# Graph layers on one core: VectorE takes part of the next pair's columns later, the normalisation moves to the second tile, and two copies change places

## The chip, the cores and the metric

The kernel runs on one core of one Trainium2 chip, as one program. The metric is the time of that program on the device, in microseconds (us). The kernel before takes 2264.59 us (median of 3 runs, 2262.41 to 2264.99).

The core's engines are TensorE (PE in the profile, with PEld for its weight loads), VectorE (DVE), ScalarE (ACT), GpSimd (POOL) and SyncE (SP). Each runs its own instructions strictly in the written order and meets the others only at semaphores. SP and POOL also issue DMA transfers. What stands in front of an instruction on its own engine delays it as much as the semaphore that it waits for.

## The reference

Four graph layers follow each other over 10,000 nodes with 512 features and 2,500 edges, each with a residual and a layer norm. Their core is:

```
x = layernorm(x + GAT(x))        # two attention layers of width 1024, then "fc": h @ Wfc + bfc
x = layernorm(x + conv(x))       # relu(segment_sum((x @ W)[src] * edge_weight, dst))
x = layernorm(x + painn(x))      # messages on edges, softplus, two small products
x = layernorm(x + mlp(x))        # relu(concat(x[src], x[dst]) @ W.T + b), summed by src
```

The last three layers change only rows that an edge touches. All other rows of their output are layer norms of layer norms of the first layer's row.

## The kernel before

All nodes stand in 79 tiles of 128 rows, and two tiles make a pair (`m` in the code, one `s = m % 2` for its buffers). The second attention layer and the fc product with its norm are one long function, `node_layers`. The part that the change touches is the last third: a loop over 79 tiles `u`, which each of the five engines writes out for itself. In each tile PE makes the fc product in 8 slices `k` of three matmuls (lines 2653 to 2655, each operand split in a high and a low part, `x_hi` and `x_lo`). After each slice stands `beside(g)` with `g = 8u + k`: a table of positions, on each engine, at which the three edge layers are worked off beside the fc product. A conv step comes every 5 slices from tile 43 to tile 57, a painn step every 5 slices (in two parts, the second 3 slices later) from tile 58 to tile 74, and the mlp weights follow up to tile 78. The mlp layer itself runs after the loop.

What each engine does for the fc product and its norm:

- **Columns of the next pair.** From tile 40 on, the fc input of a pair comes ready for use from memory (`x_in`). ACT rounds a quarter of it to the high part (`round_columns`, line 2736, rows `g_x_hi<-g_x_in`) and DVE subtracts to get the low part (`split`, line 2930, rows `g_x_lo<-g_x_in`). Four such quarters `f` are made for pair m+1 while PE works at pair m. `fills(h)` puts all four in the first tile of pair m, at slices 0, 2, 4 and 6, on both engines. PE waits for all four low parts at the start of pair m+1, and SP loads new columns into the buffer when they are done.
- **Sum and statistics.** At the end of each tile DVE adds the residual rows (`add_rows`, line 3036, rows `fc_z`) and takes the statistics (3038). PE may start tile u+2 only after the addition of tile u. At the end of a pair DVE makes the variances (`spread`, 3046 to 3053).
- **Norm of the pair before.** In the first tile of pair m, ACT makes the reciprocal roots (`root`, lines 2797 and 2799) at slice 2, DVE the shifts (`results`, line 3060, and for pairs with edges also `y`, line 3070) at slice 2, and ACT the scaled rows at slice 7: two instructions of `normalize` (2808) for the 20 pairs with edges, or two of `finish_y` (2819) for the others.

A conv step (for edge tile n) on the engines: PE multiplies tile n (`product`, 1254 to 1256), turns n+1 and sums n+2. ACT at the same position rounds the turned sums of n+1 (`conv_t_hi`, 1284) and copies the sums of n+2 (1272, 1276). DVE adds tile n (`conv_z`, 1328), makes the low part of n+1 (`conv_t_lo`, 1349), and then statistics and variances of n (1332 to 1343). Three slices later ACT makes the root (1289, 1291), DVE the shift (`conv_shift`, 1355, 1356) and ACT three scaled rows (1301, 1302, 1304: `conv_x` twice and `conv_y`). PE's product of n+1 in the next step waits for `conv_t_lo` of n+1.

A painn step: in its first part PE makes features (1485, into the same PSUM tile as the sums, so only after ACT has copied these), ACT copies them (1552), DVE makes a mask (1628) and three message products (1640 to 1644) and, in every second step, `scalars` (1654) from the softplus. In its second part PE makes products and sums the edges (1496); ACT copies the hidden rows (1588), the turned rows (1544), in every second step the softplus (three instructions, 1596 to 1600), and then the edge sums (`copy_sums`, 1567, rows `painn_sums`).

Of the kernel before, what the change touches and what calls it, by code (L numbers as in the profile page):

```python
# [33 lines left out]
ET = -(-E // P)  # L34
# [11 lines left out]
S_X2DST, S_X2SRC, S_X3SRC, _, S_X3DST, S_OUT, S_EDGE = range(7)  # L46
# [1864 lines left out]
def node_layers(nc, sem, held, h1, al1, scan_row, row_d, row_s, map_d, map_s, slot_tab, b1, avec, h2, h2_cols, al2, bounce1, bounce2,  # L1911
# [67 lines left out]
    def takes_columns(m):  # L1979
        return m >= GM and rest(m)  # L1980
# [17 lines left out]
    def fills(h):  # L1998

        m = halves_of[h][0]  # L2000
        if m + 1 == MACROS:
# [2 lines left out]
        return [(k, f) for i, k, f in (((0, 2, 0), (0, 6, 1), (1, 2, 2), (1, 6, 3)) if slow else  # L2004
                                       ((0, 0, 0), (0, 2, 1), (0, 4, 2), (0, 6, 3))) if first_half[m] + i == h]

    def halves_done(m):
        return first_half[m + 1] if m + 1 < MACROS else HALVES

# [3 lines left out]
    with ExitStack() as ctx:  # L2013
# [241 lines left out]
        def with_x1(m):  # L2255
            return tiles(m)[0] < ENDS
# [10 lines left out]
        with nc.Block() as block:  # L2267
# [456 lines left out]
            def _(act):  # L2724
# [100 lines left out]
                def beside(g):  # L2825
# [23 lines left out]
                    if part == 1:  # L2849
                        if 0 <= n < ET:  # L2850
                            painn.copy_hidden(act, n)
                        if 0 <= n + 2 < ET:
                            painn.copy_xt(act, n + 2)
                        if 0 <= n < ET and n % 2 == 1:
                            painn.softplus(act, n // 2)
                        if 0 <= n + 1 < ET:
                            painn.copy_sums(act, n + 1)
                        if n % 2 == 0 and 0 <= n - 4 < ET:
                            painn.own(act, n - 4)
                            painn.own(act, n - 3)  # L2860
# [19 lines left out]
                for u in range(TILES):  # L2880
                    h = GH + u
                    m = halves_of[h][0]
                    if WFC < h <= WFC + KC:
                        round_fc(h - WFC - 1)
                    for k in range(KC):
                        for after_k, f in fills(h):
                            if after_k == k:
                                relu(m + 1, f)
                        if m > GM and h == first_half[m]:
                            if k == 2:  # L2890
                                root(m - 1)
                            if k == KC - 1 and with_x1(m - 1):
                                normalize(m - 1)
                            if k == KC - 1 and not with_x1(m - 1):
                                finish_y(m - 1)
                        beside(KC * u + k)
                root(MACROS - 1)
                for n in range(-1, ET):
# [13 lines left out]
            def _(dve):  # L2912
# [169 lines left out]
                def beside(g):  # L3082
# [21 lines left out]
                        conv.shifts(dve, n)  # L3104
                    n, part = painn_part(g)
                    if part == 0:
                        if n % 2 == 0 and 0 <= n - 2 < ET:
                            painn.scalars(dve, (n - 2) // 2)
                        if 0 <= n + 1 < ET:
                            if n == -1:  # L3110
                                dve.wait_ge(painn.w_scaled, 3)
                            painn.masks(dve, n + 1)
                            painn.messages(dve, n + 1)
                        if n % 2 == 0 and 0 <= n - 4 < ET:
                            painn.shifts(dve, (n - 4) // 2)
                            painn.far(dve, n - 4)
                            painn.far(dve, n - 3)
# [43 lines left out]
                for u in range(TILES):  # L3161
# [3 lines left out]
                        rest_fc(h - WFC - 1)  # L3165
                    for k in range(KC):
                        for after_k, f in fills(h):
                            if after_k == k:
                                split(m + 1, f)
                        if m > GM and h == first_half[m] and k == 2:  # L3170
                            results(m - 1)
                        beside(KC * u + k)
                    add_rows(h)
                    if h + 1 == halves_done(m):
                        spread(m)
# [103 lines left out]
```

How the kernel before makes its waits and increments, by code:

```python
            @block.sync  # L263
# [5 lines left out]
                def store(m, s):  # L269
                    for j in node_tiles(m):
                        sp.wait_ge(evac_done, 2 + 2 * m + j + 1)
                        sp.sem_inc(passed, 1)
                        sp.dma_start(h_out[bass.ds(m * G + j * P, P), :], h_sb[2 * s + j][:, :]).then_inc(h_stored[2 * s + j], 16)
                    n = len(node_tiles(m))
                    sp.wait_ge(al_done, 32 + 16 * m + 8 * n)
                    sp.sem_inc(passed, 1)
                    sp.dma_start(al_out[bass.ds(m * G, n * P), :].rearrange("(j p) k -> p j k", p=P),
                                 al_sb[s][:, 0:n, :]).then_inc(al_stored[s], 16)
# [1 line left out]
                def loop(start, stop):  # L280
                    with sp.Fori(start, stop) as i:
                        for s in range(2):
                            m = 2 * i + s
                            sp.wait_ge(lo_done, m + 1)
                            sp.sem_inc(passed, 1)
                            load(m + 2, s)
                            store(m, s)
# [7 lines left out]
                for k in range(2, KC):  # L296
                    sp.wait_ge(w_lo_done, 2 * (k - 1))
                    sp.dma_start(w_raw[:, k % 2, :], w[k * P:(k + 1) * P, :]).then_inc(w_in[k % 2], 16)
# [1 line left out]
                def load_w2(k):  # L301
                    if k >= 2:
                        sp.wait_ge(w2_lo_done, k - 1)
                    sp.dma_start(w_raw[:, k % 2, :], w2[k * P:(k + 1) * P, :]).then_inc(w2_in[k % 2], 16)
```

## Time and profile before

| | kernel before |
|---|---|
| time, median of 3 runs | 2264.59 us (2262.41 to 2264.99) |
| time of the profiled execution | 2264.73 us |
| span in the profile | 2263.0 us |
| PE busy | 2204.2 us, 97% |
| DVE busy | 1486.6 us, 66% |
| ACT busy | 1021.1 us, 45% |
| POOL busy | 943.2 us, 42% |
| PE's granted clock, mean | 0.99 |

The profile is one execution. Times in its views are counted from the start of the span. Matmuls are pipelined and their ends are modelled, so a row of 0.39 us on PE does not mean that the next matmul started that much later: the distance of the starts is what counts. "Idle before" in brackets is the time in which the engine had nothing to run before an instruction, with what ended it. The loop over the 79 tiles starts at 1475.1 us and its last tile ends near 2111.9 us; the conv steps lie between 1739 and 1911 us, the painn steps between 1922 and 2090 us.

### The profile page before, as it was taken

The page shows a single profiled execution, that of the slowest core. Times are in us where ns is not written, and L with a number is a line of the kernel's source. Part 1 is how long each engine was busy: PE and PEld are TensorE (multiplying, and loading weights), DVE is VectorE, ACT ScalarE, POOL GpSimd, SP SyncE. Part 2 cuts the span into 40 slices and gives each one's busy share as a digit, 9 for nine tenths or more (in the row PEclk, how much of TensorE's full clock was granted, in tenths as well). Part 3 has the DMA queues.
Part 4 walks back from the last instruction along what each step waited for, and adds up shares of the span by engine and source line. Part 5 has one row for each costly group of instructions (what it writes and reads, how often), then busy time and mean ns, then how long its engine had stood idle before and what let it go on. Part 6 is the DMA issues. An engine that isn't in the chain of part 4 may idle for free.

```text
span 2263.0 us, 36380 instructions
## 1 busy us (share of the span) xinstructions
PE 2204.2 (97%) x12269; PEld 1888.9 (83%) x12269; DVE 1486.6 (66%) x4615; ACT 1021.1 (45%) x2028; POOL 943.2 (42%) x931
## 2 busy tenths in 40 slices
PE   7999999979999999999999999999999999999997
PEld 6878888858899888888999999988888777888785
DVE  7777878754666856665335665277776766678675
ACT  4982113222366632222225665334344665666454
POOL 2018637645222234366542322023545553652542
PEclk9999999989999999999999999999999999999998
DMA  6343565443476757786225666356667776776542
GB/s 213 139 139 127 155 208 190 151 136 105 139 247 229 258 171 267 265 281 238 87 88 188 220 228 242 126 191 211 230 206 256 238 242 220 240 251 225 168 121 70
DMA packets 192495, 435.82 MB, mean 193 GB/s; under 512 B 45751, under 2 KB 74622, under 8 KB 191774
## 3 DMA queue, kind: packets, MB, share of 16 engines
q1 hardware_dynamic: 127034, 249.08, 31.8%
q0 software_dynamic: 65296, 184.67, 26.1%
q8 instruction: 89, 1.46, 0.3%
q14 instruction: 76, 0.62, 0.1%
HBM read 242.68 MB, written 190.96 MB: 192 GB/s over the span
## 4 chain that ended last, share of the span: by engine, by line
PE 70%; DVE 4%; ACT 2%; issue 2%; DMA 1%; POOL 0%; POOLq 0%; ACTq 0%; DVEq 0%; SPq 0%
PE g_h_ps L2611 7%; PE g_h_ps L2628 7%; PE g_h_ps L2613 7%; PE g_h_ps L2612 7%; PE g_h_ps L2629 6%; PE g_h_ps L2630 6%; PE g_h_ps L2653 5%; PE g_h_ps L2655 5%; PE g_h_ps L2654 5%; PE g_t_ps L80 4%; PE g_h_ps L1783 2%; PE g_h_ps L1785 2%; PE g_h_ps L1784 2%; PE g_sum_ps L1023 1%; PE g_sum_ps L1022 1%
## 5 line engine op out<-in xcount | busy, mean ns | idle before, releaser
L2750 ACT ACTIVATE g_act_t<-g_t_ps,g_b_col 128x256 f32<-128x256 f32 (+1 forms) x488 | 201.9, 466 | 395.0 <-PE g_t_ps L80 394.8
L2628 PE MATMUL g_h_ps<-g_x_hi,held_w_hi 128*128 128x256 f32 x1216 | 352.1, 290 | 0.0
L2629 PE MATMUL g_h_ps<-g_x_lo,held_w_hi 128*128 128x256 f32 x1216 | 343.9, 283 | 0.0
L2630 PE MATMUL g_h_ps<-g_x_hi,held_w_lo 128*128 128x256 f32 x1216 | 343.7, 283 | 0.0
L632 DVE CUSTOM_DVE_ANT_0 g_prod<-g_h_sb,g_a_rows 128x256 f32<-128x256 f32 x632 | 224.3, 420 | 84.7 <-ACT g_h_sb L513 75.6
L2653 PE MATMUL g_h_ps<-fc_w_hi,g_x_hi 128*128 128x512 f32 x632 | 268.4, 425 | 3.3 <-DVE fc_z L3036 2.5
L2611 PE MATMUL g_h_ps<-held_w_hi,g_x_hi 128*128 128x512 f32 x656 | 263.7, 402 | 0.0
L2612 PE MATMUL g_h_ps<-held_w_lo,g_x_hi 128*128 128x512 f32 x656 | 256.8, 391 | 0.0
L2613 PE MATMUL g_h_ps<-held_w_hi,g_x_lo 128*128 128x512 f32 x656 | 256.8, 391 | 0.0
L2655 PE MATMUL g_h_ps<-fc_w_hi,g_x_lo 128*128 128x512 f32 x632 | 247.3, 391 | 0.0
L441 PE MATMUL g_h_ps<-g_w_hi,g_x_hi 128*128 128x512 f32 x616 | 243.0, 395 | 3.9 <-DVE g_x_lo L618 2.0
L2654 PE MATMUL g_h_ps<-fc_w_lo,g_x_hi 128*128 128x512 f32 x632 | 246.7, 390 | 0.0
L442 PE MATMUL g_h_ps<-g_w_lo,g_x_hi 128*128 128x512 f32 x616 | 242.1, 393 | 0.0
L443 PE MATMUL g_h_ps<-g_w_hi,g_x_lo 128*128 128x512 f32 x616 | 241.9, 393 | 0.0
L2629 PEld LDWEIGHTS g_h_ps<-g_x_lo,held_w_hi 128*128 128x128 f32 x1216 | 232.7, 191 | 0.1
L2630 PEld LDWEIGHTS g_h_ps<-g_x_hi,held_w_lo 128*128 128x128 f32 x1216 | 232.7, 191 | 0.0
L2628 PEld LDWEIGHTS g_h_ps<-g_x_hi,held_w_hi 128*128 128x128 f32 x1216 | 232.4, 191 | 0.1
L2928 DVE CAST g_x_hi<-g_act_t 128x512 fp32r<-128x512 f32 (+1 forms) x244 | 104.4, 428 | 194.0 <-ACT g_act_t L2750 192.5
L513 ACT ACTIVATE g_h_sb<-g_h_ps 128x1024 f32<-128x1024 f32 x79 | 81.1, 1027 | 246.2 <-PE g_h_ps L443 231.4
L2946 DVE CUSTOM_DVE_ANT_0 g_prod<-g_h_sb,g_a_rows 128x256 f32<-128x256 f32 x320 | 116.7, 419 | 98.5 <-ACT g_h_sb L2770 98.4
L2930 DVE TENSOR_TENSOR g_x_lo<-g_act_t,g_x_hi 128x512 fp32r<-128x512 f32 (+1 forms) x244 | 168.3, 690 | 8.4
L2442 POOL DMA_INDIRECT g_x_in<-h,held_perm x99 | 100.5, 1016 | 173.5 <-PE g_t_ps L80 101.6
(401 smaller groups left out, 4839.4 us busy)
## 6 DMA issues: line engine op xcount, KB each, us to landing
h<-g_h_sb SPq DMA_DIRECT2D x120, 512.0 KB, 3.8
h<-g_rows_own SPq DMA_DIRECT2D x40, 512.0 KB, 4.8
g_x_in<-in_dram SPq DMA_DIRECT2D x39, 512.0 KB, 3.9
h_cols<-g_h_sb SPq DMA_DIRECT2D x38, 512.0 KB, 3.7
xb_rows<-in_dram SPq DMA_DIRECT2D x19, 1024.0 KB, 5.4
xb<-xb_rows SPq DMA_DIRECT2D x19, 1024.0 KB, 4.4
g_x_in<-h_cols SPq DMA_DIRECT2D x38, 512.0 KB, 6.9
g_x_in<-h SPq DMA_DIRECT2D x21, 512.0 KB, 5.5
```

Of the source, the lines that this page charges most:

```text
L441: pe.matmul(out, xh, wh, start=(k == 0), stop=False)
L442: pe.matmul(out, xh, wl, start=False, stop=False)
L443: last = pe.matmul(out, xl, wh, start=False, stop=(k == KC - 1))
L2611: pe.matmul(out, xh, wh, start=(k == 0), stop=False)
L2612: pe.matmul(out, xh, wl, start=False, stop=False)
L2613: last = pe.matmul(out, xl, wh, start=False, stop=(k == KC - 1))
L2628: pe.matmul(out, wh, xh, start=(k == 0), stop=False)
L2629: pe.matmul(out, wh, xl, start=False, stop=False)
L2630: last = pe.matmul(out, wl, xh, start=False, stop=(k == KC - 1))
L2653: pe.matmul(out, xh, fc_hi[:, k, :], start=(k == 0), stop=False)
L2654: pe.matmul(out, xh, fc_lo[:, k, :], start=False, stop=False)
L2655: last = pe.matmul(out, xl, fc_hi[:, k, :], start=False, stop=(k == KC - 1))
```

## The change

Four things move; no operation is added or taken away. Line numbers after the first hunk grow by 14.

```diff
+    def rest_of_columns(h):
+        m = halves_of[h][0]
+        if m + 1 == MACROS or not takes_columns(m + 1):
+            return []
+        return [(k, f) for i, k, f in ((0, 4, 0), (0, 6, 1), (1, 0, 2), (1, 2, 3)) if first_half[m] + i == h]
+
+    def finishes(h):
+        m, j, _ = halves_of[h]
+        if m == GM or j + 1 < len(units(m)):
+            return None
+        return 2 if j else KC - 1
...
 (ACT, painn part 1)
+                        if 0 <= n + 1 < ET:
+                            painn.copy_sums(act, n + 1)
                         if 0 <= n < ET and n % 2 == 1:
                             painn.softplus(act, n // 2)
-                        if 0 <= n + 1 < ET:
-                            painn.copy_sums(act, n + 1)
...
 (ACT, in each slice)
-                        if m > GM and h == first_half[m]:
-                            if k == 2:
-                                root(m - 1)
-                            if k == KC - 1 and with_x1(m - 1):
-                                normalize(m - 1)
-                            if k == KC - 1 and not with_x1(m - 1):
-                                finish_y(m - 1)
+                        if m > GM and h == first_half[m] and k == 4:
+                            root(m - 1)
+                        if k == finishes(h) and with_x1(m - 1):
+                            normalize(m - 1)
+                        if k == finishes(h) and not with_x1(m - 1):
+                            finish_y(m - 1)
                         beside(KC * u + k)
...
 (DVE, painn part 0: scalars now behind masks and messages)
...
 (DVE, in each slice)
                         for after_k, f in fills(h):
+                            if after_k == k and not takes_columns(m + 1):
+                                split(m + 1, f)
+                        if m > GM and h == first_half[m] and k == 6:
+                            results(m - 1)
+                        beside(KC * u + k)
+                        for after_k, f in rest_of_columns(h):
                             if after_k == k:
                                 split(m + 1, f)
-                        if m > GM and h == first_half[m] and k == 2:
-                            results(m - 1)
-                        beside(KC * u + k)
```

So DVE makes the low parts at slices 4 and 6 of the first tile and 0 and 2 of the second, four slices behind ACT's rounding, and behind the edge work of the slice. The root moves from slice 2 to 4, the results from 2 to 6, and the scaled rows from slice 7 of the first tile to slice 2 of the second. The instructions of PE, POOL and SP stand in the same order as before.

On DVE, at the end of tile 53 and in the first slices of tile 54 (`g_ds` ends the variances of the pair, `g_x_lo` are the low parts for the pair of tiles 56 and 57, `conv_*` belong to the edge work), the order before is:

```order
L3053 SCALAR_TENSOR_TENSOR g_ds_4251<-g_ds_4251,g_mv_4249 128x2 x3
L2930 TENSOR_TENSOR g_x_lo_4199<-g_x_in_4192,g_x_hi_4197 128x512
L1355 SCALAR_TENSOR_TENSOR conv_shift_4287<-conv_mv_4279,conv_rstd_4285 128x2
L1356 SCALAR_TENSOR_TENSOR conv_shift_4287<-conv_mv_4279,conv_rstd_4285 128x1
L2930 TENSOR_TENSOR g_x_lo_4199<-g_x_in_4192,g_x_hi_4197 128x512
L3060 SCALAR_TENSOR_TENSOR g_shift_4257<-g_mv_4249,g_rstd_4255 128x2 x2
L1319 TENSOR_SCALAR conv_weighted_4275<-g_mask,held_tabs 128x128
L1328 SCALAR_TENSOR_TENSOR conv_z_4269<-g_misc_ps,conv_x_dst 128x512
L1349 TENSOR_TENSOR conv_t_lo<-g_sum_ps,conv_t_hi 128x512
```

And after the change the same stretch, with the rows up to the second low part:

```order
L3066 SCALAR_TENSOR_TENSOR g_ds_4251<-g_ds_4251,g_mv_4249 128x2 x3
L1355 SCALAR_TENSOR_TENSOR conv_shift_4287<-conv_mv_4279,conv_rstd_4285 128x2
L1356 SCALAR_TENSOR_TENSOR conv_shift_4287<-conv_mv_4279,conv_rstd_4285 128x1
L1319 TENSOR_SCALAR conv_weighted_4275<-g_mask,held_tabs 128x128
L1328 SCALAR_TENSOR_TENSOR conv_z_4269<-g_misc_ps,conv_x_dst 128x512
L1349 TENSOR_TENSOR conv_t_lo<-g_sum_ps,conv_t_hi 128x512
```

Both low parts and the results have left the stretch between the variances and `conv_t_lo`; the first low part now comes after the statistics that follow.

At the end of tile 54 and in the first slices of tile 55 DVE now has:

```order
L3049 TENSOR_TENSOR fc_z_4242<-g_h_ps,g_a_rows 128x512
L3051 BN_STATS g_stats_4248<-fc_z_4242 128x6
L2943 TENSOR_TENSOR g_x_lo_4199<-g_x_in_4193,g_x_hi_4197 128x512
L1355 SCALAR_TENSOR_TENSOR conv_shift_4287<-conv_mv_4279,conv_rstd_4285 128x2
L1356 SCALAR_TENSOR_TENSOR conv_shift_4287<-conv_mv_4279,conv_rstd_4285 128x1
L2943 TENSOR_TENSOR g_x_lo_4199<-g_x_in_4193,g_x_hi_4197 128x512
```

The last two low parts of the pair now stand behind the addition of the first tile (`fc_z`), in the second tile.

On ACT, in tiles 52 and 53 (`fc_y` are the scaled rows of the pair before, `g_log_d` and `g_rstd` its root), the order before is:

```order
L2736 ACTIVATE g_x_hi_4198<-g_x_in_4195 128x512 x2
L1289 ACTIVATE conv_log_d_4283<-conv_ds_4281 128x3
L1291 ACTIVATE conv_rstd_4285<-conv_log_d_4283 128x3
L1301 ACTIVATE conv_x_4262<-conv_z_4270,conv_shift_4287,conv_rstd_4285 128x512
L1302 ACTIVATE conv_x_4262<-conv_x_src,conv_shift_4287,conv_rstd_4285 128x512
L1304 ACTIVATE conv_y_4268<-conv_z_4270,conv_shift_4287,conv_rstd_4285 128x512
L2819 ACTIVATE fc_y_4244<-fc_z_4242,g_shift_4258,g_rstd_4256 128x512 x2
L1284 ACTIVATE conv_t_hi<-g_sum_ps 128x512
```

And after:

```order
L2811 ACTIVATE g_log_d_4254<-g_ds_4252 128x4
L2813 ACTIVATE g_rstd_4256<-g_log_d_4254 128x4
L2750 ACTIVATE g_x_hi_4198<-g_x_in_4195 128x512
L1289 ACTIVATE conv_log_d_4283<-conv_ds_4281 128x3
L1291 ACTIVATE conv_rstd_4285<-conv_log_d_4283 128x3
L1301 ACTIVATE conv_x_4262<-conv_z_4270,conv_shift_4287,conv_rstd_4285 128x512
L1302 ACTIVATE conv_x_4262<-conv_x_src,conv_shift_4287,conv_rstd_4285 128x512
L1304 ACTIVATE conv_y_4268<-conv_z_4270,conv_shift_4287,conv_rstd_4285 128x512
L1284 ACTIVATE conv_t_hi<-g_sum_ps 128x512
L1272 ACTIVATE conv_x_src<-g_sum_ps 1x512
L1276 ACTIVATE conv_sums<-g_sum_ps 128x512
L2833 ACTIVATE fc_y_4244<-fc_z_4242,g_shift_4258,g_rstd_4256 128x512 x2
```

The scaled rows left the place in front of `conv_t_hi` and stand behind the copies of the next conv step; the root came between the two last roundings.

## Rows read from the trace of the kernel before

**Rows 1.** Waits of PE: what waited for what, us in total, times, longest.
```profile
PE g_h_ps L1254 <- DVE conv_t_lo L1349: 4.6, 3, 2.1
...
PE g_sum_ps L1485 <- ACT painn_sums L1567: 3.0, 6, 0.7
PE g_h_ps L2653 <- DVE fc_z L3036: 2.5, 1, 2.5
...
PE g_t_ps L80 <- DVE mlp_t_lo L1861: 1.8, 2, 1.0
```

**Rows 2.** Stretches: us, busy (instructions) by engine, PEclk, DMA share, GB/s.
```profile
1850.00:1912.00 62.00, 57.83 (x252) 44.29 (x250) 40.39 (x127) 37.25 (x75) 21.76 (x22) 1.00 0.62 210
```

**Rows 3.** Waits of all engines, columns as in rows 1.
```profile
DVE g_x_lo L2930 <- ACT g_x_hi L2736: 28.9, 15, 3.0
```

**Rows 4.** DVE in order of time, tile 54: start, us, instruction, [idle before].
```profile
1877.20 0.69 DVE L2930 TENSOR_TENSOR g_x_lo<-g_x_in,g_x_hi 128x512 fp32r<-128x512 f32 x1
1877.81 0.15 DVE L1355 SCALAR_TENSOR_TENSOR conv_shift<-conv_mv,conv_rstd 128x2 f32<-128x2 f32 x1
...
1880.95 0.69 DVE L2930 TENSOR_TENSOR g_x_lo<-g_x_in,g_x_hi 128x512 fp32r<-128x512 f32 x1 [2.92 <-ACT g_x_hi L2736]
...
1882.50 0.68 DVE L1349 TENSOR_TENSOR conv_t_lo<-g_sum_ps,conv_t_hi 128x512 fp32r<-128x512 f32 x1
```

**Rows 5.** ACT in order of time, the same stretch.
```profile
1878.07 0.81 ACT L1301 ACTIVATE conv_x<-conv_z,conv_shift,conv_rstd 128x512 f32<-128x512 f32 x1 [3.14 <-DVE conv_shift L1356]
...
1880.21 0.62 ACT L2736 ACTIVATE g_x_hi<-g_x_in 128x512 fp32r<-128x512 f32 x1
...
1881.06 0.58 ACT L1284 ACTIVATE conv_t_hi<-g_sum_ps 128x512 fp32r<-128x512 f32 x1
```

**Rows 6.** PE in order of time: two early conv products, one late, one pair start.
```profile
1748.99 0.39 PE L1254 MATMUL g_misc_ps<-conv_w_hi,conv_t_hi 128*128 128x512 f32 x1
...
1756.45 0.39 PE L1254 MATMUL g_h_ps<-conv_w_hi,conv_t_hi 128*128 128x512 f32 x1
...
1883.24 0.50 PE L1254 MATMUL g_h_ps<-conv_w_hi,conv_t_hi 128*128 128x512 f32 x1 [1.86 <-DVE conv_t_lo L1349]
...
1896.87 0.40 PE L2653 MATMUL g_h_ps<-fc_w_hi,g_x_hi 128*128 128x512 f32 x1
```

**Rows 7.** ACT in order of time, end of tile 52.
```profile
1863.40 1.51 ACT L2819 ACTIVATE fc_y<-fc_z,g_shift,g_rstd 128x512 f32<-128x512 f32 x2
1864.82 0.58 ACT L1284 ACTIVATE conv_t_hi<-g_sum_ps 128x512 fp32r<-128x512 f32 x1
```

**Rows 8.** DVE in order of time: tiles 53, 54 and 56.
```profile
1865.43 0.69 DVE L1349 TENSOR_TENSOR conv_t_lo<-g_sum_ps,conv_t_hi 128x512 fp32r<-128x512 f32 x1 [2.08 <-ACT conv_t_hi L1284]
...
1871.70 0.69 DVE L1349 TENSOR_TENSOR conv_t_lo<-g_sum_ps,conv_t_hi 128x512 fp32r<-128x512 f32 x1 [1.76 <-ACT conv_t_hi L1284]
...
1893.45 0.69 DVE L3036 TENSOR_TENSOR fc_z<-g_h_ps,g_a_rows 128x512 f32<-128x512 f32 x1
...
1912.17 0.69 DVE L2930 TENSOR_TENSOR g_x_lo<-g_x_in,g_x_hi 128x512 fp32r<-128x512 f32 x1 [2.91 <-ACT g_x_hi L2736]
1912.78 0.68 DVE L3036 TENSOR_TENSOR fc_z<-g_h_ps,g_a_rows 128x512 f32<-128x512 f32 x1
```

**Rows 9.** The chain that ended last, 1904 to 1926 us: start, us, what.
```profile
1910.01 0.81 ACT conv_x L1302
...
1915.60 7.17 DMA painn_u<-u_tab,g_side_out
...
1922.81 0.33 PE g_sum_ps L1469
```

**Rows 10.** One stretch behind PE's longest conv wait, columns as in rows 2.
```profile
1834.40:1837.60 3.20, 3.20 (x9) 2.49 (x8) 3.03 (x12) 1.86 (x5) 2.08 (x2) 0.50 0.73 228
```

**Rows 11.** ACT in order of time: a softplus with its copy, and one root.
```profile
1985.63 0.40 ACT L1596 ACTIVATE painn_soft<-painn_hid_s 128x256 f32<-128x256 f32 x1
...
1986.93 0.42 ACT L1567 ACTIVATE painn_sums<-g_sum_ps 128x320 f32<-128x320 f32 x1
...
2023.77 0.21 ACT L2797 ACTIVATE g_log_d<-g_ds 128x4 f32<-128x4 f32 x1 [2.63 <-DVE g_ds L3053]
```

More of the change, by code:

```diff
@@ L3106, in beside @@
                     if part == 0:
-                        if n % 2 == 0 and 0 <= n - 2 < ET:
-                            painn.scalars(dve, (n - 2) // 2)
                         if 0 <= n + 1 < ET:
@@ L3113, in beside @@
                             painn.messages(dve, n + 1)
+                        if n % 2 == 0 and 0 <= n - 2 < ET:
+                            painn.scalars(dve, (n - 2) // 2)
                         if n % 2 == 0 and 0 <= n - 4 < ET:
```

## Prediction

> **What bounds the kernel now.** I read first what PE waits for, then the busy times by stretch, then DVE and ACT in order of time at PE's longest waits, and last the chain that ended last. PE bounds the kernel: even in the stretch with most waiting, 1850 to 1912 us, it is busy 57.83 of 62 us [rows 2]. So only PE's waits and its clock can be won, and the reader should price those first. In the part that the change touches they are four sums [rows 1]: 4.6 us for `conv_t_lo`, 3.0 us in six pieces for `painn_sums`, 2.5 us once for `fc_z`, 1.8 us twice for `mlp_t_lo`. A fifth is the clock: behind the longest conv wait (2.1 us [rows 1]) a stretch of 3.2 us ran at a granted clock of 0.50, the 1.2 GHz level [rows 10], so PE did there what takes half the time at 2.4 GHz, and 1.6 us were lost. Together 4.6 + 3.0 + 2.5 + 1.8 + 1.6 = 13.5 us, 0.6% of the time: no forecast may give more.
>
> Why PE waits is seen at tile 54. DVE made a low part at 1877.20 and only then the shift of the conv step at 1877.81. ACT's three scaled rows started on that shift (1878.07, after 3.14 us idle), ACT's next rounding `g_x_hi` stood behind them (1880.21) and `conv_t_hi` behind that (1881.06) [rows 4, 5]. Meanwhile DVE stood 2.92 us at its second low part, which needs that rounding; two additions later came `conv_t_lo` (1882.50), and PE's product, ready at 1883.24 - 1.86 = 1881.38, began at 1883.24 [rows 4, 6]. This ping-pong is common: DVE waits 28.9 us in 15 pieces for ACT's rounding [rows 3].
>
> **The change, part by part.**
>
> *Low parts later.* In the code DVE reaches each low part four slices after ACT's place for the rounding, with one conv step between; that step's `conv_t_lo` needs `conv_t_hi`, which ACT makes after the rounding. So the wait of rows 3 can't arise there: DVE will find the rounding done. At tile 54 the shift comes 0.61 us sooner (1877.81 - 1877.20), ACT's rows and `conv_t_hi` with it, which also loses the root in front of it (two small instructions). `conv_t_hi` ended at 1881.06 + 0.58 = 1881.64 and would end by 1881.03; DVE, idle by then, adds 0.68 and PE starts near 1881.7 or sooner: about 0.3 of 1.86 us are left.
>
> *Scaled rows later.* At tile 53 `fc_y` took ACT from 1863.40 to 1864.82 just in front of `conv_t_hi`, and DVE's `conv_t_lo` at 1865.43 waited for that [rows 7, 8]. This 1.42 us now stands in the second tile, mostly between a conv step and its variances, where ACT is idle for DVE. But it does not fall so at each phase. With nothing else between, one conv step follows another on the DVE-ACT chain in 1871.70 - 1865.43 = 6.27 us [rows 8]; PE takes 1756.45 - 1748.99 = 7.46 us for one [rows 6]. So a step has 1.19 us to spare. From the table of slices, two steps (tiles 46 and 48, each at the first tile's end) get two or three low parts of 0.61 us and the 1.42 us in one loop, 2.6 to 3.3 us; in between the lag runs down again. I leave 1.0 us of conv waits for these, and take 3.6 of 4.6 us (bounds 0, if all recur, and 4.6).
>
> *Clock.* The half-rate stretch followed the 2.1 us wait; the wait of 1.86 us had none, the mean clock of its stretch being 1.00 [rows 1, 2, 6]. With no wait over 1 us I expect none: 1.6 us (bounds 0 and 1.6). The Trainium skill (TensorE: Matmul & The Clock Gate, Part 1: The HAM clock gate) says that how many matmuls run at the low level differs between runs of one kernel. By that rule the dip could also return behind shorter waits, and the sum below would be 8.4 instead of 10.0; rows 10 show one dip in one execution and decide nothing between the two.
>
> *The 2.5 us for `fc_z`.* At tile 56 DVE stood 2.91 us at the last low part (1912.17), with `fc_z` behind it (1912.78), which PE needs for tile 58 [rows 1, 8]. That low part is now in tile 57, so the wait goes. What is late next is known: the first painn step needs gathers that POOL issues only when the last conv rows are stored. `conv_x` ran at 1910.01, the gather of 7.17 us started at 1915.60, and PE used it at 1922.81, as soon as it was there [rows 9]. If PE comes 2.5 us sooner, this chain must too. Its shift stood behind two more low parts and the results than it will, 1.2 us at least; 2.5 at most. I take 1.9 us (bounds 0 and 2.5).
>
> *Sums ahead of the softplus, scalars behind the messages.* The softplus took 1986.93 - 1985.63 = 1.30 us in front of `painn_sums` [rows 11], more than the longest of PE's six waits there, 0.7 us [rows 1]. Another copy stood behind a root that waited 2.63 us for the variances [rows 11]; that root is now two slices later, behind this copy. What is late instead is the softplus, by one copy of 0.42 us, and `scalars`, by four short DVE instructions; both are used by PE only in the second part, three slices on. I take 2.6 of 3.0 us (bounds 0 and 3.0).
>
> *mlp.* Its weights come in round trips that start when the last painn rows are stored, so PE and that chain come forward together. One low part of 0.61 us leaves DVE's queue ahead of the last painn shift: 0.3 of 1.8 us (bounds -0.5, for the scaled rows that now stand among the weights' roundings, and 1.8).
>
> *Queues and the other stages.* SP's loads wait for the low parts and go out up to a tile later, and stand at most that much in front of its stores; they are needed two tiles on. POOL's scatter of `y` waits for the scaled rows and has the conv and painn gathers behind it; a gather is issued three steps (22 us by rows 6) before PE needs it, and POOL is at PE's pace. In the 38 tiles before, where the scaled rows have the same move, PE waits for nothing of this (the waits of [rows 1] are the only ones in the loop of over 1 us in sum), and the second tile of a pair has no other use for ACT: 0.
>
> Sum: 3.6 + 1.6 + 1.9 + 2.6 + 0.3 = 10.0 us. The profiled execution took 2264.73 us for a span of 2263.0; it stands 0.14 above the median of 2264.59. So 2264.6 - 10.0 = 2254.6 us, 0.44% faster. Less than 0.2% (4.5 us) can't be told from no change.
>
> **The rivals.**
>
> *Half comes back.* The scaled rows meet the conv chain at the wrong phase: half of the 4.6 stays, with a wait long enough for the clock dip, and the gather chain keeps the 2.5. For it: the spare of 1.19 us per step is thin [rows 6, 8], and PE took the gather the moment it came [rows 9]. Against it: low parts and scaled rows are now spread over both tiles. Gain 2.3 + 2.6 + 0.3 = 5.2: 2259.4 us. Chance 0.20.
>
> *The waits only move.* PE arrives sooner and stands at the next transfer or ACT copy, as each stall of this kernel was set by a chain that itself follows PE. Between no gain and 4 us: about 2262.5 us. For it: rows 9; against: in rows 4 and 5 the delay is a queue order, not a distance. Chance 0.13.
>
> *Slower: the low parts come too late for the pair.* PE needs all four at the start of a pair, and two of them now stand behind `fc_z` of the first tile. At tile 54 `fc_z` came at 1893.45, and PE began the next pair at 1896.87 [rows 6, 8]: 3.42 us, in which now the addition and its statistics (2 x 0.7), a shift and two low parts (2 x 0.61) must fit, 2.8 us. It decides if DVE lags 0.6 us more than before. Then PE waits at most of the 18 pair starts from tile 42 on, say 1 us at each and the clock dip of 1.6 at a quarter: 18 + 7 = 25 us against 10, so 2264.6 + 15 = 2280 us; with 0.7 us at each and no dip 2267. Against it: with the 2.9 us stands gone DVE should lag less. Chance 0.11.
>
> **How the numbers follow.** The forecast has 0.56, with 2251 to 2257.5 as its own range (all terms whole give 2251.1; the conv and gather terms halved 2257.4). Faster by over 0.2% is the forecast, 0.56, and nearly all of the first rival, 0.18: 0.74. Within 0.2%: the second rival and the rest of the first, 0.15. Slower: 0.11. The range goes from 2250.0 (all terms and 1 us for the spread of the runs, 2262.41 to 2264.99) to 2262.5, where half of the second rival and the third are left out.
>
> **What would show it.** Right: no wait of DVE for `g_x_hi` in conv steps; PE's waits for `conv_t_lo` about 1 us and for `painn_sums` under 0.5; no stretch at 0.50 between 1740 and 2120 us; PE's wait before the first painn step under 1 us. Wrong: PE waiting for `g_x_lo` at pair starts, ACT's `conv_t_hi` behind `fc_y` in a second tile, or a wait of 2 us for the painn gather.

## The result and the profile after

The changed kernel takes 2248.93 us (median of 4 runs, 2245.87 to 2250.0), the kernel before beside it 2263.5 us: ratio 0.9928 [0.9916, 0.994]. That is 14.6 us by the medians and 16.3 us by the ratio (which is not that of the medians), where 10.0 us were forecast. The direction was right; the time fell 1.1 us below the predicted range, which began at 2250.0 us. The profiled execution took 2249.59 us for a span of 2247.9 us.

PE's waits in the changed kernel, as in [rows 1] (what waited for what, us in total, times, longest):

```profile
PE g_h_ps L2667 <- DVE g_x_lo L2943: 2.1, 2, 1.3
...
PE g_t_ps L80 <- DVE mlp_t_lo L1861: 1.6, 2, 1.0
...
PE g_sum_ps L1469 <- DMA painn_u<-u_tab,g_side_out: 0.4, 1, 0.4
PE g_h_ps L1254 <- DVE conv_t_lo L1349: 0.3, 1, 0.3
```

(L2667 and L2943 are L2653 and L2930 of the kernel before: DVE's lines have grown by 13, not by 14.) The 4.6 us for `conv_t_lo` are 0.3, and the rows for `painn_sums` and `fc_z` are gone. The 0.4 us for a gather are those of the third painn step; the first, which [rows 9] named as next, costs PE 0.06 us here and 0.34 in the second profile of the changed kernel.

All signs that the prediction named for being right are there, and two of those for being wrong, both small. One is new in the list: 1.3 us for a low part at a pair start. The other is `conv_t_hi` behind `fc_y` in a second tile on ACT, at three places. The last of them, in tile 49, stands ahead of the one conv wait that is left on PE:

```profile
1811.16 1.51 ACT L2833 ACTIVATE fc_y<-fc_z,g_shift,g_rstd 128x512 f32<-128x512 f32 x2
1812.57 0.58 ACT L1284 ACTIVATE conv_t_hi<-g_sum_ps 128x512 fp32r<-128x512 f32 x1
```

```profile
1813.92 0.50 PE L1254 MATMUL g_h_ps<-conv_w_hi,conv_t_hi 128*128 128x512 f32 x1 [0.35 <-DVE conv_t_lo L1349]
```

Where the time went is read from the starts of PE's fc products, first in the kernel before (the loop's first; tiles 57, 58, 74 and 78):

```profile
1475.08 0.50 PE L2653 MATMUL g_h_ps<-fc_w_hi,g_x_hi 128*128 128x512 f32 x1 [0.73 <-DVE g_x_lo L2930]
...
1905.46 0.39 PE L2653 MATMUL g_h_ps<-fc_w_hi,g_x_hi 128*128 128x512 f32 x1
...
1913.61 0.47 PE L2653 MATMUL g_h_ps<-fc_w_hi,g_x_hi 128*128 128x512 f32 x1 [2.55 <-DVE fc_z L3036]
...
2082.75 0.47 PE L2653 MATMUL g_h_ps<-fc_w_hi,g_x_hi 128*128 128x512 f32 x1
...
2106.17 0.46 PE L2653 MATMUL g_h_ps<-fc_w_hi,g_x_hi 128*128 128x512 f32 x1
```

The same five products in the changed kernel:

```profile
1472.53 0.50 PE L2667 MATMUL g_h_ps<-fc_w_hi,g_x_hi 128*128 128x512 f32 x1 [0.72 <-DVE g_x_lo L2943]
...
1895.21 0.39 PE L2667 MATMUL g_h_ps<-fc_w_hi,g_x_hi 128*128 128x512 f32 x1
...
1900.85 0.50 PE L2667 MATMUL g_h_ps<-fc_w_hi,g_x_hi 128*128 128x512 f32 x1
...
2066.19 0.47 PE L2667 MATMUL g_h_ps<-fc_w_hi,g_x_hi 128*128 128x512 f32 x1
...
2091.23 0.46 PE L2667 MATMUL g_h_ps<-fc_w_hi,g_x_hi 128*128 128x512 f32 x1
```

Stage by stage, as distances between these rows:

| stage | before | after | won | forecast |
|---|---|---|---|---|
| loop start to tile 57 (conv, clock) | 430.38 | 422.68 | 7.7 | 3.6 + 1.6 |
| tile 57 to 58 (`fc_z`) | 8.15 | 5.64 | 2.5 | 1.9 |
| tile 58 to 74 (painn) | 169.14 | 165.34 | 3.8 | 2.6 |
| tile 74 to 78 (a low part for tile 76) | 23.42 | 25.04 | -1.6 | 0 |
| together | 631.09 | 618.70 | 12.4 | 9.7 |

The other 0.3 us of the forecast were for `mlp_t_lo`, whose waits lie behind tile 78: their 1.8 us became 1.6 here and 0.9 in the second profile. Between two executions of one kernel the stages shift against each other, the sums hardly: the kernel before, profiled again, has 429.2, 7.7, 170.5 and 23.6 us, together 631.08; the changed one, again, 423.1, 5.6, 164.9 and 25.0, together 618.69.

The loop's first product came 2.55 us sooner, behind code that the change doesn't touch. The stretch of all conv and painn steps, in the kernel before and then in the changed one (columns as in [rows 2]):

```profile
1740.00:2110.00 370.00, 358.88 (x1791) 289.07 (x1790) 259.18 (x763) 230.80 (x515) 189.54 (x190) 1.00 0.72 239
```

```profile
1740.00:2110.00 370.00, 365.68 (x1846) 297.35 (x1845) 267.95 (x788) 238.50 (x530) 193.79 (x194) 1.00 0.73 243
```

PE is busy for 365.68 instead of 358.88 of 370 us, and every other engine is busier too: the same 370 us hold more of the work (1846 instead of 1791 matmuls). A part of that is only the earlier start of the loop.

The mechanism is seen on DVE. The group of low parts made from `x_in`, in the changed kernel (busy us, mean ns, idle before): no idle time is left where [rows 3] had 28.9 us.

```profile
L2943 DVE TENSOR_TENSOR g_x_lo<-g_x_in,g_x_hi 128x512 fp32r<-128x512 f32 x76 | 51.1, 681 | 0.0
```

And DVE at tile 54, where [rows 4] had the ping-pong:

```profile
1869.54 0.15 DVE L1355 SCALAR_TENSOR_TENSOR conv_shift<-conv_mv,conv_rstd 128x2 f32<-128x2 f32 x1
...
1869.87 0.69 DVE L1328 SCALAR_TENSOR_TENSOR conv_z<-g_misc_ps,conv_x_dst 128x512 f32<-128x512 f32 x1
1873.06 0.69 DVE L1349 TENSOR_TENSOR conv_t_lo<-g_sum_ps,conv_t_hi 128x512 fp32r<-128x512 f32 x1 [2.50 <-ACT conv_t_hi L1284]
```

PE's product of that step:

```profile
1874.06 0.39 PE L1254 MATMUL g_h_ps<-conv_w_hi,conv_t_hi 128*128 128x512 f32 x1
```

DVE still stands, now at `conv_t_lo` itself, but that comes 3.52 us behind the shift (1873.06 - 1869.54) instead of 4.69 us (1882.50 - 1877.81 [rows 4]), and PE, which waited 1.86 us here [rows 6], waits no more.

### The profile page after: what moved, and what is told of

It is laid out like the page before. It is cut to its first block, busy times and chain, and to the rows that moved or that the text cites. A ratio compares the mean times of both kernels' runs of the same rounds, so it can differ in the third digit from the quotient of the medians.

```text
span 2247.9 us, 36380 instructions
## 1 busy us (share of the span) xinstructions
PE 2199.6 (98%) x12269; PEld 1888.6 (84%) x12269; DVE 1487.8 (66%) x4615; ACT 1024.2 (46%) x2028; POOL 937.4 (42%) x931
## 4 chain that ended last, share of the span: by engine, by line
PE 72%; DVE 2%; DMA 1%; ACT 1%; issue 1%; POOL 0%; POOLq 0%; SPq 0%; ACTq 0%; DVEq 0%
PE g_h_ps L2625 7%; PE g_h_ps L2642 7%; PE g_h_ps L2627 7%; PE g_h_ps L2626 7%; PE g_h_ps L2643 6%; PE g_h_ps L2644 6%; PE g_h_ps L2667 6%; PE g_h_ps L2669 5%; PE g_h_ps L2668 5%; PE g_t_ps L80 4%; PE g_h_ps L1783 2%; PE g_h_ps L1785 2%; PE g_h_ps L1784 2%; PE g_sum_ps L1023 1%; PE g_sum_ps L1022 1%
## 5 line engine op out<-in xcount | busy, mean ns | idle before, releaser
L2667 PE MATMUL g_h_ps<-fc_w_hi,g_x_hi 128*128 128x512 f32 x632 | 268.8, 425 | 2.1 <-DVE g_x_lo L2943 2.1
L2943 DVE TENSOR_TENSOR g_x_lo<-g_act_t,g_x_hi 128x512 fp32r<-128x512 f32 (+1 forms) x244 | 168.6, 691 | 8.4
L2456 POOL DMA_INDIRECT g_x_in<-h,held_perm x99 | 95.7, 967 | 173.4 <-PE g_t_ps L80 101.5
```

The lines of the kernel that those rows point to most:

```text
L2667: pe.matmul(out, xh, fc_hi[:, k, :], start=(k == 0), stop=False)
```

## The experiments

Each kernel ran beside the kernel before on the same chip. F is the distance from the loop's first fc product to the end of the span, in the one profile of each row; it leaves out the unchanged code ahead, whose end lay between 1472.5 and 1479.6 us in these profiles. The last three columns are PE's waits: for `conv_t_lo` (both PSUM targets), for `painn_sums`, and for low parts at tile starts (0.7 of them at the loop's first product in all).

| kernel | median us | ratio to before | F | conv | painn | low parts |
|---|---|---|---|---|---|---|
| before (first profile) | 2263.5 | | 788.0 | 5.1 | 3.0 | 0.7 |
| before, as control | 2264.69 | 0.9997 [0.9988, 1.0007] | 788.1 | 5.0 | 3.0 | 0.7 |
| changed | 2248.93 | 0.9928 [0.9916, 0.994] | 775.4 | 0.3 | 0 | 2.1 |
| changed, again | 2251.27 | 0.9937 [0.9925, 0.9949] | 774.7 | 0.7 | 0 | 2.0 |
| low parts only | 2255.86 | 0.9954 [0.994, 0.9967] | 781.0 | 2.7 | 1.4 | 2.6 |
| normalisation only | 2263.62 | 0.9993 [0.9983, 1.0004] | 785.8 | 5.1 | 1.0 | 0.7 |
| painn edits only | 2263.7 | 0.9987 [0.9977, 0.9996] | 787.4 | 5.3 | 0.9 | 0.7 |
| low parts, scaled rows | 2252.32 | 0.9945 [0.9924, 0.9965] | 778.5 | 1.5 | 1.4 | 2.6 |
| low parts, root, results | 2254.77 | 0.9956 [0.9941, 0.997] | 779.2 | 2.2 | 0.6 | 2.0 |
| low parts, normalisation | 2252.62 | 0.994 [0.9927, 0.9953] | 776.9 | 0.4 | 0.7 | 2.0 |
| low parts, painn edits | 2255.85 | 0.9955 [0.9942, 0.9967] | 780.5 | 2.7 | 1.0 | 2.6 |
| low parts later still | 2258.58 | 0.997 [0.996, 0.998] | 785.1 | 0 | 0 | 9.1 |
| one low part sooner | 2251.18 | 0.9941 [0.9928, 0.9954] | 774.3 | 0.4 | 0 | 0.7 |
| that, and the mlp pair first | 2249.17 | 0.9933 [0.9917, 0.995] | 771.8 | 0.4 | 0 | 0.7 |

**One part at a time.** The kernel before with `rest_of_columns` and its use on DVE alone:

```diff
                         for after_k, f in fills(h):
-                            if after_k == k:
+                            if after_k == k and not takes_columns(m + 1):
                                 split(m + 1, f)
...
                         beside(KC * u + k)
+                        for after_k, f in rest_of_columns(h):
+                            if after_k == k:
+                                split(m + 1, f)
```

> Only the low parts move (slices 4 and 6 of the first tile, 0 and 2 of the second); root, results, scaled rows and the painn order stay as before. Theory of the queue order: DVE's 28.9 us of waits for ACT's rounding fall under 5 us, the long conv waits (2.15 and 1.86 us), the half-clock stretch near 1834 us and the 2.5 us wait for fc_z go; the waits behind fc_y (0.60, 0.51) and those behind the softplus stay; a new wait for a low part of 1 to 1.5 us comes before tile 76. Counted by the distance of starts: 2.3 + 1.7 + 2.0 + 2.7 - 0.5 (gather) + 0.7 - 1.4 = 7.5 us less than before. Rival, the waits only move: under 3 us less. Rival, parts not additive because any relief of the DVE-ACT loop is enough: 10 us or more less.

10.4 us less by the ratio (interval 7.5 to 13.6) and 7.0 by F: F fits the theory's 7.5, and the ratio can't tell it from the second rival's 10 or more. DVE's waits for ACT's rounding are gone, as expected. PE's waits:

```profile
PE g_h_ps L2660 <- DVE g_x_lo L2937: 2.6, 2, 1.8
PE g_h_ps L1254 <- DVE conv_t_lo L1349: 2.2, 2, 1.5
...
PE g_sum_ps L1485 <- ACT painn_sums L1567: 1.4, 3, 0.7
```

So the low parts also took half of the painn waits, which the prediction put down to the softplus and the root, and half of the conv waits stayed: of the two long ones, which the theory had both going, 1.5 us are left at tile 54. DVE shows why. It now runs on to the next instruction that needs ACT, the shifts of `results`, and stands there for the root, which on ACT stands behind the next rounding:

```profile
DVE g_shift L3067 <- ACT g_rstd L2806: 12.8, 12, 3.2
```

In the kernel before this wait is 1.0 us in sum, in the changed kernel 1.8. It stands in front of `conv_t_lo` on DVE just as the low parts did. With root and results later and `finishes`, the low parts as before:

```diff
-                            if k == 2:
+                            if k == 4:
                                 root(m - 1)
...
-                            if k == KC - 1 and with_x1(m - 1):
+                        if k == finishes(h) and with_x1(m - 1):
                             normalize(m - 1)
...
-                        if m > GM and h == first_half[m] and k == 2:
+                        if m > GM and h == first_half[m] and k == 6:
                             results(m - 1)
```

> Only the norm of the pair before moves (root to slice 4, results to 6, scaled rows to slice 2 of the second tile); low parts and the painn order stay. Theory of the queue order: the conv waits behind fc_y (0.60, 0.51) and the painn waits behind the root (0.50, 0.74) and fc_y (0.19, part of 0.65) go, the waits behind the low parts (2.15, 1.86 us) and the 2.5 us for fc_z stay: 3 to 4 us less than before. Whether the half-clock stretch comes back behind a wait of about 2 us tells if it hangs on that wait. Rival, not additive: 8 us or more less.

A miss for conv: its waits add up to 5.1 us as before, only partly at the same places. 1.6 us less by the ratio and 2.2 by F, where 3 to 4 were expected; the painn waits fell to 1.0 us, about as expected. Behind the wait of 2.0 us a stretch at 0.50 came again, behind the 2.5 us for `fc_z` none.

```profile
PE g_h_ps L1254 <- DVE conv_t_lo L1349: 4.9, 4, 2.0
...
PE g_h_ps L2660 <- DVE fc_z L3043: 2.5, 1, 2.5
...
PE g_sum_ps L1485 <- ACT painn_sums L1567: 1.0, 2, 0.5
```

With `copy_sums` ahead of the softplus and `scalars` behind the messages alone:

```diff
+                            painn.copy_sums(act, n + 1)
                         if 0 <= n < ET and n % 2 == 1:
                             painn.softplus(act, n // 2)
-                        if 0 <= n + 1 < ET:
-                            painn.copy_sums(act, n + 1)
```

> Only the two exchanges in the painn steps (sums ahead of the softplus, scalars behind the messages). Theory: of PE's six waits for painn_sums the four behind a softplus go or shrink (0.46, 0.41 and most of 0.65 and 0.19), the two behind a root (0.50, 0.74) stay: by distance of starts 1.5 to 2.5 us less than before; conv waits, clock stretch and fc_z wait as before. Rival, the waits only move (PE then stands at out_two for the later scalars): no change.

The painn waits fall from 3.0 to 0.9 us: those behind a softplus are gone, as expected, and one of the two behind a root stays. A wait of 0.75 us is new, once, at L1533, the product in a step's second part that needs the scalars, and ends just after DVE's `scalars`: the rival, at one step. The ratio gives 2.9 us [0.9 to 5.2], F 0.6 us. By the starts tiles 58 to 74 took 1.7 us less, although a stretch at half clock fell into them (1914.7 us), and tiles 74 to 78 took 0.8 us more, with a wait of 0.6 us for a copy of ACT that the first profile has not. The control is the kernel before, unchanged:

> The kernel before, unchanged, profiled once more. Theory that the first 1475 us (unchanged code) differ from execution to execution by their clock stretches and small waits: the loop over the tiles starts anywhere between 1471 and 1476 us here and in the three other kernels, with no relation to the edit; the loop itself takes the same 636 us to within 0.5. Rival, the edit also makes the first part shorter: the loop starts at 1475.1 within 0.5 here and in kernels without the change, and near 1472.5 with it.

Its ratio is 0.9997. The loop starts at 1474.67 us and is as long as in the first profile to 0.02 us, as the theory said. (One later kernel, low parts with painn edits, started its loop at 1479.6 us, outside 1471 to 1476.) The profile also shows the clock's part in one kernel's spread: two stretches at 0.50 where the first profile had one [rows 10], and none behind the wait that had it there.

```profile
1882.50:1885.60 3.10, 3.10 (x9) 2.37 (x8) 1.49 (x8) 1.88 (x5) 0.00 (x0) 0.50 0.37 118
1913.10:1916.30 3.20, 3.20 (x9) 2.42 (x9) 3.03 (x12) 1.61 (x5) 2.38 (x3) 0.50 0.97 331
1832.90:1836.00 3.10, 3.10 (x15) 2.51 (x16) 2.96 (x11) 1.77 (x5) 2.49 (x3) 1.00 0.69 213
```

**The change again, and all but one part.** The changed kernel, not edited:

> The changed kernel once more. In the profiles so far the unchanged code ahead of the loop over the 79 tiles ended anywhere from 1472.5 to 1476.7 us, and the first profile of the changed kernel was the one with 1472.5. Theory: that 2.5 us is no part of the change; the loop itself (first fc product to the last tile) is 12.4 us shorter, so the time is 12 to 13 us below the kernel before on the same chip, ratio 0.9940 to 0.9950. Rival: the whole 14.6 us belong to the change: ratio 0.993, and the loop starts at 1473 or sooner again.

The loop up to tile 78 is as short as in the first profile to 0.01 us (it starts at 1475.62 us this time), so 12.4 us are the loop's, and the sooner start of the first profile is no part of the change. But the ratio gives 14.3 us [11.6 to 17.0], between the theory's 12 to 13 and the rival's 14.6, so the times confirm neither. The changed kernel without the painn edits (the first two diffs together):

> Later low parts and later normalisation together, without the painn edits. Alone, the low parts left 2.2 us of PE's waits for conv_t_lo, and the normalisation alone left 4.9. Theory (the two hide each other: each removes one of two works in front of conv_t_hi): together under 0.6 us of conv waits, no stretch at half clock in the conv steps, and the painn waits of 1.4 us of the low parts alone stay; 12 us less than before, ratio 0.9945 to 0.9955. Rival (parts only add): conv waits near 2, 9 us less, ratio 0.996.

```profile
PE g_t_ps L80 <- DVE mlp_t_lo L1861: 1.5, 1, 1.5
PE g_sum_ps L1485 <- ACT painn_sums L1567: 0.7, 2, 0.5
...
PE g_h_ps L1254 <- DVE conv_t_lo L1349: 0.4, 1, 0.4
```

The theory holds for conv: low parts leave 2.7, the normalisation alone leaves 5.1 of 5.1, both together 0.4. The painn waits are 0.7 instead of the 1.4 expected: the normalisation stood in front of `painn_sums` too. The changed kernel without the normalisation (the first diff and the third):

> Later low parts and the painn edits, with the normalisation at its old places. Theory: conv waits stay at 2.2 us as with the low parts alone, painn_sums under 0.3; 11 us less than before, ratio 0.995. Rival (the normalisation matters for the conv waits only through the painn steps or not at all): conv waits under 0.6 and a time like that of the whole change.

```profile
PE g_h_ps L1254 <- DVE conv_t_lo L1349: 2.2, 2, 1.5
PE g_sum_ps L1485 <- ACT painn_sums L1567: 1.0, 1, 1.0
```

Conv stays at 2.7, as expected; for `painn_sums` one wait of 1.0 was left, where under 0.3 was expected. It goes only when the normalisation moves too.

Which half of the normalisation does it? The low parts with `finishes` but root and results at slice 2, and the other way round:

> Later low parts with the scaled rows in the second tile, but root and results at their old places, and no painn edits. Theory (the scaled rows are what stood in front of conv_t_hi beside the low parts): conv waits of PE under 0.7 us in sum instead of 2.7 with the low parts alone, no stretch at half clock in the conv steps; loop of 624 us. Rival (the root and the results did it): conv waits stay at 2 or more, loop of 628 or more.

```profile
PE g_h_ps L1254 <- DVE conv_t_lo L1349: 1.2, 2, 0.7
PE g_misc_ps L1254 <- DVE conv_t_lo L1349: 0.3, 1, 0.3
```

> Later low parts with the root two slices and the results four slices later, the scaled rows in the first tile's last slice as before, and no painn edits. Theory (the scaled rows matter, not these): conv waits stay at 2 us or more, as with the low parts alone (2.7). Rival: they fall under 0.7.

```profile
PE g_h_ps L1254 <- DVE conv_t_lo L1349: 1.7, 3, 0.7
...
PE g_misc_ps L1254 <- DVE conv_t_lo L1349: 0.5, 1, 0.5
```

Neither theory as a whole: 1.5 and 2.2 us stay, against 2.7 with neither and 0.4 with both. Each takes a share (1.2 and 0.5), and the last 0.6 goes only with both. (The second kernel's 2.2 us do meet the bound of its theory, 2 or more; that the scaled rows alone matter does not hold.) DVE's wait for the root is still 12.8 us in the first of these kernels and 1.8 in the second.

**The deadline.** The changed kernel with its last two low parts two slices later:

```diff
-        ... ((0, 4, 0), (0, 6, 1), (1, 0, 2), (1, 2, 3)) ...
+        ... ((0, 4, 0), (0, 6, 1), (1, 2, 2), (1, 4, 3)) ...
```

> The changed kernel with the third and fourth low part of each pair two slices later still (slices 2 and 4 of the second tile instead of 0 and 2). In the changed kernel the last low part ends between 0.05 and 5.7 us before PE starts the pair, at 6 of 18 pairs less than 2.6 us. Two slices are 1.4 us of PE without edge work between them and 3 to 6 us with a step. Theory (the spare is as thin as it looks, and the slower rival of the prediction starts here): PE waits for g_x_lo at 5 or more pair starts, 8 us in all or more, and the time is 8 us or more over the changed kernel, 2259 us or above. Rival (VectorE runs ahead where it may): at most two such waits, under 3 us more.

```profile
PE g_h_ps L2667 <- DVE g_x_lo L2943: 9.1, 5, 2.8
```

7.3 us over the changed kernel by the medians (2258.58 - 2251.27, from two comparisons), 10 by F; the expected 2259 was missed by 0.4. Without the loop's first product four pair starts wait, 8.4 us in all, instead of five or more; the longest wait is 2.8 us, with a granted clock of 0.50 at two of them:

```profile
1796.10:1799.30 3.20, 3.20 (x9) 2.52 (x8) 2.07 (x9) 2.46 (x4) 1.37 (x2) 0.50 0.86 168
1895.10:1901.70 6.60, 5.80 (x14) 4.54 (x15) 3.08 (x12) 4.49 (x10) 2.58 (x3) 0.50 0.67 224
```

This is the mechanism of the slower rival, two slices away from the change, at four of 18 pair starts. Even so the kernel is 0.3% faster than the kernel before.

**The new wait.** DVE in the changed kernel before tile 76, then PE:

```profile
2075.02 0.68 DVE L2943 TENSOR_TENSOR g_x_lo<-g_x_in,g_x_hi 128x512 fp32r<-128x512 f32 x1
2077.32 0.69 DVE L1853 TENSOR_TENSOR mlp_w_lo<-fc_w_raw,mlp_w_hi 128x512 fp32r<-128x512 f32 x1 [1.63 <-ACT mlp_w_hi L1805]
2077.93 0.68 DVE L2943 TENSOR_TENSOR g_x_lo<-g_x_in,g_x_hi 128x512 fp32r<-128x512 f32 x1
```

```profile
2078.67 0.50 PE L2667 MATMUL g_h_ps<-fc_w_hi,g_x_hi 128*128 128x512 f32 x1 [1.33 <-DVE g_x_lo L2943]
```

The pair's last low part stands behind the first mlp weight, which waits for ACT. One slice sooner for this pair alone, it stands ahead of it:

```diff
-        ... (1, 2, 3)) ...
+        ... (1, 2 if takes_columns(m + 2) else 1, 3)) ...
```

> The changed kernel with one low part, the last one for the pair of tiles 76 and 77, one slice sooner, so ahead of the first mlp weight on VectorE instead of behind it. Both theories: the 1.33 us wait of PE for g_x_lo at tile 76 goes. Theory A (a wait is worth its distance): 1.5 us less than the changed kernel. Theory B (the end of the loop is set by the loads of the mlp weights, which follow the last painn store and not PE): PE comes to the mlp pair 1.4 us sooner and waits there, the 0.6 us for mlp_t_lo become 2.0, and the time stays within 0.5 us. I expect B.

The rows fit theory B: the wait is gone, and after its last fc tile PE now waits 1.37 us for the mlp pair, where the changed kernel had 0.63 in one profile and no wait in the other. The time stays (2251.18 against 2251.27), but intervals of some 6 us could not show theory A's 1.5 us. PE's wait, and then the next kernel, which has the first mlp pair rounded and split ahead of the eighth weight, on ACT and likewise on DVE:

```diff
+                    if g == FIRST_PAIR:
+                        mlp.round_pair(act, 0)
                     if r == 0 and 0 <= k < mlp.KC:
                         ...
                         mlp.round_w(act, k)
-                    if g == FIRST_PAIR:
-                        mlp.round_pair(act, 0)
```

```profile
PE g_t_ps L80 <- DVE mlp_t_lo L1861: 2.3, 2, 1.4
```

> The kernel with the last low part for tile 76 sooner, in which PE waits 1.37 us for mlp_t_lo after its last fc tile, now with the rounding and the split of the first mlp pair ahead of the eighth mlp weight on ScalarE and VectorE. Theory (the pair stood behind a weight that came late): this wait goes, 1.4 us less than that kernel and than the changed kernel, 0.06%, seen in PE's rows (last fc tile to the end of the span) more than in the times. Rival: PE waits as long for the weight itself, in its first mlp product: 0.

```profile
PE g_t_ps L80 <- DVE mlp_t_lo L1861: 0.8, 1, 0.8
```

The 1.37 us are gone and F is 771.8, 2.5 us less than with the low part alone and 2.9 to 3.5 less than the changed kernel. That is more than the 1.4 expected, but the part behind tile 78 differs by up to 2.2 us among the profiles of the other kernels, which are alike there; so the size is not shown. By the times it is not told apart from the changed kernel (0.9933 against 0.9928 and 0.9937, intervals of 0.002 and more).

## Why the prediction was right in direction and wrong in size

- **The term that was mis-sized most is conv: 3.6 us forecast, 6.1 measured** (7.7 less the 1.6 of one stretch at half clock [rows 10]: tile 51, which holds it, took 17.55 us from its first fc product to the next tile's, and 15.99 in the control, where the same wait had no such stretch). The step that failed is the price of a wait: I took "idle before" as what a wait costs. PE at the 1.86 us wait of [rows 6], with the product ahead of it and the one behind:

```profile
1880.99 0.39 PE L2655 MATMUL g_h_ps<-fc_w_hi,g_x_lo 128*128 128x512 f32 x1
1883.24 0.50 PE L1254 MATMUL g_h_ps<-conv_w_hi,conv_t_hi 128*128 128x512 f32 x1 [1.86 <-DVE conv_t_lo L1349]
1883.57 0.40 PE L1255 MATMUL g_h_ps<-conv_w_lo,conv_t_hi 128*128 128x512 f32 x1
```

  The starts are 2.25 us apart where 0.23 is usual, so 2.02 are lost, and the next start is 0.33 behind instead of 0.23: 2.12, not 1.86. A matmul's row is 0.39 long, and its tail past 0.23 counts as busy though the next could have started. Four waits at 0.26 more, and the 0.5 us for `g_misc_ps` that I left out, make 4.6 + 0.5 + 1.0 = 6.1 (an estimate: the 0.3 that stay are not taken off, and delays too short for the list not added). Whole tiles show the same price: tile 54, with the wait of 1.86 us, took 15.25 us and takes 13.10 in both profiles of the changed kernel; tile 55, with the 0.51, took 9.88 and takes 9.08. So of the 2.5 us by which the term was too small, about 1.0 is the price, 0.5 the row left out, and the rest the reserve of the next point. The Trainium skill (TensorE: Matmul & The Clock Gate, Part 2: What happens when you issue a matmul) says that back-to-back matmuls hide each other's drain and a single one can't; these rows agree.
- **The share of conv that I thought would come back** (1.0 us, from the spare of 1.19 us a step) was 0.3 in one profile and 0.7 in the other. The scaled rows do meet conv at the wrong phase, but at one place only, right behind tile 48, one of the two that the prediction named (the rows of ACT above); the wait there is all that came back. The reason given, works out of the front of `conv_t_hi`, is shown by the single parts, which leave 2.7 and 5.1 us, and 0.4 together. What the working did not have is that DVE, freed of its stand at the low parts, would stand for the root instead unless the results move too: at tile 54 the working came to 0.3 us left, with the root out of the way, and with the low parts alone 1.5 us are left.
- **Clock: right for the changed kernel** (no stretch at 0.50 in its loops in both profiles), but the one dip that the term counts is one draw of the kernel before, whose control has two at other waits. From the first fc product to the first mlp products of all 14 profiles 10 of the 17 waits of 1.8 us or more were followed by one, and 1 of the 10 waits of 1.3 to 1.5.
- **`fc_z`: 1.9 forecast, 2.5 measured.** The gather chain did come forward with PE, and by more than the term asked: the first gather was issued at 1903.27 instead of 1915.60, and PE used it at 1910.06 instead of 1922.81 [rows 9]. POOL and PE in the changed kernel:

```profile
1903.27 0.94 POOL L1454 DMA_INDIRECT painn_u<-u_tab,g_side_out  x1 [0.30 <-issue]
```

```profile
1910.06 0.33 PE L1469 MATMUL g_sum_ps<-g_ident,painn_x 128*128 128x128 f32 x1
```

  The wait at tile 58 hung on the low part in front of `fc_z`, and nearly all of it was won.

- **painn: 2.6 forecast, 3.8 measured**, the same mis-pricing: six waits of 3.0 us idle and 0.16 more by the starts are 4.0. The cause was named too narrowly: low parts, root and results, without the painn edits, leave 0.6 us.
- **mlp: 0.3 forecast, 0.2 and 0.9 measured** by the waits for `mlp_t_lo` in the two profiles. **Put at nothing, and measured at -1.6: the low part for tile 76.** I counted the low part that leaves the queue, and not that another one now stands behind a weight that waits. So PE waited as in the slower rival, at one pair start of 18, but not for the rival's reason: not `fc_z` stood in front, but the mlp weight.
- **"No forecast may give more than 13.5"** was wrong as a bound for the same reason: by the starts the four sums and the clock are 6.1 + 4.0 + 2.8 + 2.1 + 1.6 = 16.6, an estimate (0.26 a wait, 0.16 for painn's and mlp's).

The stages as measured make 12.4 us in the loop, and F gives 12.6 to 13.4. The medians differ by 14.6 and 14.55 us, the ratios by 16.3 [13.6 to 19.0] and 14.3 [11.6 to 17.0]: the second interval holds the loop's 12.4, the first does not. What the other 1 to 4 us are stays open. The unchanged code ahead of the loop varies by more than that, and two profiles can't say how often the kernel before drops its clock. The loop's 12.4 us alone would have ended near 2252.2 us, inside the predicted range, as the second comparison's 2251.27 did; so the mis-sized terms explain why the gain was over 10.0 us, and the open rest is what carried the first comparison out of the range.

## What to carry to other kernels

Price a wait of PE by the distance of the starts on both sides of it, not by its idle time, and sum all rows that wait for the same instruction, also the small ones of another target. Where two works stand in front of a waited-for instruction, trying one alone says little: here they left 2.7 and 5.1 of 5.1 us, and 0.4 together. Ask at which instruction the freed engine will stand next; here it was the one right behind in the same queue. For work moved later, list what stands in front of its new place in every iteration, the last one above all, where other stages begin.

## What the runs showed of the hardware

The same kernel drops to half clock at different waits in different executions: behind a wait of 2.1 us in the first profile, and behind waits of 1.9 and 2.1 us, not that one, in the control. In the stretches at 0.50, 9 matmuls stand in 3.2 us, against 15 in 3.1 us at 1.00. A dip can be given back: from the first fc product to the last, both loops of the kernel before are 635.9 us long, with one dip and with two. By the starts of the fc products, the dip behind the wait of 1.9 us made tile 54 of the control 1.6 us longer than in the first profile, and tiles 55 to 57 were 1.6 us shorter: the wait of 0.5 us at tile 55 is gone and that for `fc_z` is 2.1 instead of 2.5 us (what shortened tile 56 the list of waits does not show). The Trainium skill (TensorE: Matmul & The Clock Gate, Part 1: The HAM clock gate) says that the number of slow matmuls at a kernel's start differs between runs of it. These two profiles show such a difference in the middle of a kernel.
